# Parting the two gathers of a unit, and turning the last y term by term

## The chip, the cores and the metric

The kernel runs on one core of one Trainium2 chip. The metric is the device time of a whole execution in microseconds; the median of three runs stands for a kernel.

## The reference, cut to what matters

Input x has 32 batches of 512 rows with 256 numbers. The output is x plus a state-space layer plus a mixture of experts, both on the normalised rows xn.

```python
xn = layernorm(x)                                     # [32, 512, 256]
# state-space layer, N = 16 states, L = 512 steps
delta, B, C = split(xn @ W_deltaBC.T, [64, 80])
delta = softplus(delta @ W_dt.T + b_dt)               # [32, 512, 256]
h[t, n] = exp(delta[t] * A[n]) * h[t-1, n] + delta[t] * B[t, n] * xn[t]
y[t] = sum over n of h[t, n] * C[t, n]  +  D * xn[t]
# mixture of experts: each of 8 experts takes its best K = 128 rows of each batch
G, I = top_k(softmax(xn @ Wg.T) transposed, 128)
ex = xn[I]                                            # gather
out_e = G * (gelu(ex @ W1 + b1) @ W2 + b2)
result = x + y + scatter_add(out_e at I)
```

## The kernel before, in words

A first stage normalises the rows, writes them to HBM (`xn_rows`), projects them, and picks each expert's 128 rows of every batch. Then a main loop runs over 32 batches. Each batch is cut into 4 units (quarters 0 to 3, `sl` in the code) of `STEPS` = 4 states; so there are 128 units u. In each unit the state-space work on 4 states of one batch and the expert work on one pair of row sets (`UB` = 2, that is 2 x 128 rows of one expert) go on side by side. Each engine has its own instruction list in a fixed order, tied to the others by semaphores.

- **DVE** (`main`, lines 997 to 1008): for each state a scan over time (`tensor_tensor_scan`), then the multiply `du` x B of the next state into `bank_x` (L936, `multiply_b`), then the product of this state's h with C into `prod` (L1008). The products of states 4 and 8 are POOL's (L573).
- **POOL**: adds each product into `ysum` (L585, at most some states behind the DVE; a product buffer is free again when its sum is done), forms `delta` (L517) and `du` (L523) for the next batch in quarter 3, issues the gathers of unit u+3 (`gather`, L509), the two scatters of unit u-1 (`scatter`, L540) and the addition of a finished batch's y to the output (`add_y`, L554). The rows of an issued gather land in `ex[:, u % 2]`.
- **PE**: in unit u, with v = u+1 and a counter q from 0 to 7: up products of unit v (`up`, L1163) at q = 0 to 3; at q = 3, ahead of `up(v, 3)`, `chosen_columns(v + 1, ...)` (L1082) turns the gathered rows of unit u+2 into `bank_t`, and waits for both gathers of it; down products of unit u (L1229) at q = 4 to 7. At q = 4 and q = 6 it spreads B over the partitions for the states 4sl+3 and 4sl+4 (L1116, `spread_b`). It turns the y of the batch before (`y_rows`, L1110), the xn rows (L1090) and the rank product (L1073).
- **ACT**: copies B for the states 4sl+1 and 4sl+2 into `bank_b` (L748), scales the experts' output (`og`, L757), gelus (L726, pairs 0 to 3), copies the turned rows to `ext` (L741, between pairs 2 and 3, waiting for `chosen_columns`), exp and ln of the softplus in quarter 2 (L697, L701), and the `decay` factors of the next unit (L717).
- **SP**: loads C for the next unit (`c_all`), B (`b_wide`), weights, xn rows, with `held(...)` waits in a fixed order.

The end: in the unit behind the last one (u = `NU`) PE turns the y of the last batch in two halves of 16 matmuls each, four terms per tile (`ysum`, `kept`, `skip` and the last product), into `bank_t` and `bank_x`; ACT and DVE copy one half each, POOL adds it to the output. The order on POOL within the last unit is written out by hand in `main`.

Of the kernel before, what the change touches and what calls it, by code (L numbers as in the profile page):

```python
# [35 lines left out]
P = 128  # L36
# [42 lines left out]
def build(nc, x, wdbc, wdt, bdt, alog, dpar, wg, w1, b1, w2, b2, out):  # L79
    ctx = ExitStack()  # L80
    with ctx:
# [371 lines left out]
        def _(pool):  # L453
# [50 lines left out]
            def gather(u):  # L504

                wait(pool, ex_tr, u - 1)
                pool.wait_ge(picks_done, 2 + u // 64 * 2)
                for i in range(UB):
                    pool.indirect_dma_start(  # L509
                        out=ex[:, u % 2, i], out_offset=None, in_=xn_rows,  # L510
                        in_offset=bass.IndirectOffsetOnAxis(ap=idx_all[:, u * UB + i:u * UB + i + 1], axis=0),
                    ).then_inc(gathered[u % 2], 16)
# [12 lines left out]
            for v in range(2):  # L525
                gather(v)
            take_delta(1, 0)
            take_du(1, 0, 16)
            gather(2)
# [26 lines left out]
            def main(j):  # L556
                for k in range(BU):
# [6 lines left out]
                    for i in range(STEPS):  # L564
# [25 lines left out]
                        if i == 0:  # L590
                            if there(u + 3, NU):
                                gather(u + 3)
# [5 lines left out]
                        if i == 2 and u == NU - 1:  # L598
                            scatter(u, 1)
                            scatter(u, 0)  # L600
# [229 lines left out]
        def _(dve):  # L830
# [184 lines left out]
            nc.vector.tensor_copy(yrow[:, (NB - 1) % 2, 2:4], bank_x[:, 0, 0:T].rearrange("p (c d) -> p c d", c=2)).then_inc(yrow_done, 1)  # L1015
# [3 lines left out]
        def _(pe):  # L1019
# [79 lines left out]
            def y_rows(par, half, last=False):  # L1099

                into = bank_x[:, 0, 0:T] if last and half else bank_t[:]
                for c in (2 * half, 2 * half + 1):
                    for dt in range(HC):
                        part = into[:, (c % 2) * D + dt * P:(c % 2) * D + (dt + 1) * P]
                        rows = slice(c * P, (c + 1) * P)
                        terms = [ysum[:, par, dt, rows], kept[:, par, dt, rows], skip[:, par, dt, rows]]
                        if last:
                            terms.append(prod[:, STEPS - 1, dt, rows])
                        for t, term in enumerate(terms):
                            o = nc.tensor.matmul(part, term, ident[:], start=(t == 0), stop=(t == len(terms) - 1), is_transpose=True)  # L1110
                o.then_inc(y_tr, 1)

# [60 lines left out]
            def main(j):  # L1173
                for k in range(BU):
# [3 lines left out]
                    for q in range(2 * STEPS):  # L1178
# [64 lines left out]
                        if q in (5, 6) and u == NU:  # L1243
                            pe.wait_ge(yrow_done, NB * 2 - 2)
# [40 lines left out]
```

## Time and profile before

| | before |
|---|---|
| runs, median (lowest to highest) | 2426.65 us (2425.75 to 2430.33) |
| profiled execution, its own time | 2422.32 us |
| its span, first to last instruction | 2420.4 us |
| mean granted TensorE clock | 0.987 of full speed |
| busy: PE / DVE / ACT / POOL | 2286.8 / 2349.7 / 2074.3 / 2146.5 us |
| issue to landing of a gather / a scatter / y's addition | 2.8 / 5.2 / 8.5 us, medians |
| PE's waits for gathered rows at L1082 | 9.2 us, once (at 160.3 us, in the start) |

Busy time is the sum of the lengths of an engine's instructions. A timeline line reads: start, length, engine, line of the kernel, operation, what it writes and reads, how many instructions were merged, and in square brackets the idle time before it with what ended it. Lengths of neighbouring instructions overlap by some tenths, since the next one starts up while one drains. PEclk is the share of the TensorE clock's full speed of 2.4 GHz that was granted; 0.50 is the lower level of 1.2 GHz.

### The profile page before, as it was taken

What the parts mean: (1) busy time and instruction counts of PE and PEld (TensorE: products, weight loads), DVE (VectorE), ACT (ScalarE), POOL (GpSimd) and SP (SyncE); (2) the same over time, 40 slices, a digit from 0 to 9 for tenths busy, and PEclk for the clock granted to TensorE, in tenths of its full rate; (3) what the DMA queues carried; (4) which work ended last, traced back from release to release, by engine and by line L of the source; (5) the groups of instructions that cost most, each with busy time, mean ns of one, the idle gap of its engine ahead of it and who ended that gap; (6) DMA issues with size and microseconds to landing.
All of it is one profiled execution on the core that took longest, in us unless ns stands there. A gap on an engine that the chain in (4) does not pass through costs nothing. (4 is left out here: it accounts for less than half of the span.)

```text
span 2420.4 us, 33772 instructions
## 1 busy us (share of the span) xinstructions
PE 2286.8 (94%) x10756; PEld 1816.4 (75%) x10756; DVE 2349.7 (97%) x1975; ACT 2074.3 (86%) x3629; POOL 2146.5 (89%) x1235
## 2 busy tenths in 40 slices
PE   7749999999999999999999999999999999999996
PEld 4437777777777777777777777777778777777775
DVE  5799999999999999999999999999999999999997
ACT  7748889898888888988888889888898989888884
POOL 5527999999999899999999999999999999999997
PEclk9969999999999999999999999999999999999998
DMA  9967575645656565555656555565646456565444
GB/s 344 338 209 266 158 221 157 177 136 148 168 147 173 145 161 141 165 154 134 184 137 173 136 166 145 141 176 143 177 127 180 127 151 163 149 173 139 128 127 79
DMA packets 151649, 403.04 MB, mean 167 GB/s; under 512 B 19536, under 2 KB 88240, under 8 KB 134832
## 3 DMA queue, kind: packets, MB, share of 16 engines
q1 hardware_dynamic: 84208, 316.72, 38.2%
q0 software_dynamic: 66048, 83.92, 20.6%
q8 instruction: 87, 1.43, 0.2%
q14 instruction: 90, 0.74, 0.1%
q10 hardware_dynamic: 1216, 0.23, 0.0%
HBM read 323.72 MB, written 91.75 MB: 172 GB/s over the span
## 5 line engine op out<-in xcount | busy, mean ns | idle before, releaser
L585 POOL TENSOR_TENSOR ysum<-ysum,prod 128x1024 f32<-128x1024 f32 x415 | 1121.4, 2702 | 20.3 <-DVE prod L1008 12.1
L997 DVE TENSOR_TENSOR_SCAN bank_x<-decay,bank_x 128x1024 f32<-128x1024 f32 x448 | 1024.7, 2287 | 8.9 <-DVE bank_x L936 0.5
L1163 PE MATMUL bank_l<-ext,w_sb 128*128 128x256 f32 x4096 | 968.9, 384 | 28.2 <-ACT og L757 22.6
L1229 PE MATMUL bank_l<-w_sb,hid 128*128 128x256 f32 x4096 | 939.0, 382 | 0.0
L1163 PEld LDWEIGHTS bank_l<-ext,w_sb 128*128 128x128 f32 x4096 | 760.3, 191 | 166.5 <-ACT og L757 31.0
L1229 PEld LDWEIGHTS bank_l<-w_sb,hid 128*128 128x128 f32 x4096 | 767.5, 190 | 130.0 <-issue 29.0
L717 ACT ACTIVATE decay<-delta,a_sb 128x511 f32<-128x511 f32 x1024 | 641.9, 707 | 15.8 <-POOL delta L517 14.6
L936 DVE TENSOR_TENSOR bank_x<-du,bank_b 128x1024 f32<-128x1024 f32 x512 | 617.6, 1206 | 4.7 <-ACT bank_b L748 3.2
L726 ACT ACTIVATE hid<-bank_l,b_all 128x256 f32<-128x256 f32 x1024 | 431.5, 475 | 203.8 <-PE bank_l L1163 200.7
L1008 DVE TENSOR_TENSOR prod<-bank_x,c_all 128x1024 f32<-128x1024 f32 x448 | 544.9, 1216 | 0.1
L540 POOL DMA_INDIRECT out<-og,idx_all x256 | 410.0, 1601 | 43.8 <-POOL ysum L585 42.5
L509 POOL DMA_INDIRECT ex<-xn_rows,idx_all x256 | 258.5, 1010 | 109.4 <-issue 61.4
L748 ACT COPY bank_b<-b_wide 128x512 f32<-128x512 f32 x256 | 153.5, 599 | 7.2 <-DVE bank_x L936 6.2
L757 ACT ACTIVATE og<-bank_l,gate_all 128x256 f32<-128x256 f32 x256 | 105.9, 464 | 32.6 <-PE bank_l L1229 32.5
L1116 PE MATMUL bank_b<-bcs,pick 96*128 96x512 bf16 x256 | 98.5, 385 | 31.0 <-DVE bank_x L936 30.0
L717 ACT ACT_TABLE_LOAD x97 | 124.5, 1283 | 1.7
L824 ACT ACT_TABLE_LOAD x95 | 121.9, 1283 | 1.7
L573 POOL TENSOR_TENSOR prod<-zabs,c_all 128x1024 f32<-128x1024 f32 x32 | 109.5, 3421 | 0.0
L1116 PEld LDWEIGHTS bank_b<-bcs,pick 96*128 96x128 bf16 x256 | 24.8, 97 | 99.6 <-DVE bank_x L936 51.7
L573 POOL TENSOR_TENSOR kept<-kept,c_all 128x1024 f32<-128x1024 f32 x32 | 92.6, 2893 | 0.0
L1082 PE MATMUL bank_t<-ident,ex 128*128 128x128 f32 x512 | 77.3, 274 | 9.2 <-DMA ex<-xn_rows,idx_all 9.2
L741 ACT COPY ext<-bank_t 128x512 f32<-128x512 f32 x128 | 76.1, 594 | 6.1 <-PE bank_t L1082 6.1
(117 smaller groups left out, 1958.9 us busy)
## 6 DMA issues: line engine op xcount, KB each, us to landing
c_all<-bc_rows SPq DMA_DIRECT2D x128, 1024.0 KB, 5.1
b_wide<-bc_rows SPq DMA_DIRECT2D x128, 512.0 KB, 4.5
w_sb<-in_w SPq DMA_DIRECT2D x32, 1024.0 KB, 9.3
decay<-in_x SPq DMA_DIRECT2D x32, 512.0 KB, 6.8
xn_rows<-c_all SPq DMA_DIRECT2D x32, 512.0 KB, 6.5
out<-yrow POOLq DMA_DIRECT2D x32, 512.0 KB, 8.5
xr<-xn_rows SPq DMA_DIRECT2D x30, 512.0 KB, 6.0
bc_rows<-prod SPq DMA_DIRECT2D x32, 192.0 KB, 5.1
```

The costliest lines, as they stand in the source:

```text
L509: pool.indirect_dma_start(out=ex[:, u % 2, i], out_offset=None, in_=xn_rows, in_offset=bass.IndirectOffsetOnAxis(ap=idx_all[:, u * UB + i: ...
L540: pool.indirect_dma_start(out=out_rows, out_offset=bass.IndirectOffsetOnAxis(ap=idx_all[:, w * UB + c:w * UB + c + 1], axis=0), in_=og[:, ...
L573: nc.gpsimd.tensor_tensor(to, from_, c_all[:, u % 2, i][:, None, :].broadcast_to([P, HC, T]), ALU.mult).then_inc(gp_prod_done, 1)
L585: nc.gpsimd.tensor_tensor(ysum[:, m % 2], first, prod[:, i], ALU.add).then_inc(sum_done, 1)
L717: nc.scalar.activation(decay[:, par, i, dt, 1:T], delta[:, dpar_, dt, 1:T], ACT.Exp, scale=a_sb[:, dt, n:n + 1]).then_inc(decay_done, 1)
L726: nc.scalar.activation(hid[:, k % 2, f], bank_l[(pair + k) % 2][:, (f % 2) * UT:(f % 2 + 1) * UT], ACT.Gelu_apprx_tanh, bias=b1_all[:, exp ...
L748: nc.scalar.copy(bank_b[:], b_wide[:, s % STEPS - WIDE[0]]).then_inc(b_ready, 1)
L936: nc.vector.tensor_tensor(bank_x[:, s % 2].rearrange("p (c t) -> p c t", c=HC), du[:, par], bank_b[:][:, None, :].broadcast_to([P, HC, T]) ...
L997: nc.vector.tensor_tensor_scan(into, decay[:, k % 2, i].rearrange("p c t -> p (c t)"), bank_x[:, s % 2], 0.0, ALU.mult, ALU.add).then_inc( ...
L1008: nc.vector.tensor_tensor(prod[:, i], bank_x[:, s % 2].rearrange("p (c t) -> p c t", c=HC), c_all[:, u % 2, i][:, None, :].broadcast_to([P ...
L1163: i = nc.tensor.matmul(bank_l[(q + v) % 2][:, (f % 2) * UT:(f % 2 + 1) * UT], w1_sb[:, e2, hc, f * P:(f + 1) * P], ext[:, v % 2, hc], star ...
L1229: i = nc.tensor.matmul(o, hid[:, w % 2, f, c * K:(c + 1) * K], w2_sb[:, w_par, f], start=False, stop=(f == FC - 1 and c == UB - 1))
```

## The change

Three things are altered. `gather(u)` becomes `gather(u, i)` and issues one of the two gathers; in the main loop gather 0 of unit u+3 stands behind the first sum of a unit (as both did), and gather 1 behind the last sum (i = 3), ahead of `add_y` where there is one. In the last unit the scatters of the unit itself, which both stood behind sum 14, are parted: scatter 1 stands behind sum 13, scatter 0 behind sum 14. And the last y is turned term by term: `last_term` turns one term of one half, in the order skip, kept, `ysum`, last product, each term behind its own wait; the second half goes to `bank_l[0]` instead of `bank_x`, from where DVE copies it.

```diff
--- before.py
+++ after.py
@@ -501,15 +501,14 @@
             for r in range(4):
                 pool.wait_ge(rows_out[r], 16 * NB // 4)
 
-            def gather(u):
+            def gather(u, i):
 
                 wait(pool, ex_tr, u - 1)
                 pool.wait_ge(picks_done, 2 + u // 64 * 2)
-                for i in range(UB):
-                    pool.indirect_dma_start(
-                        out=ex[:, u % 2, i], out_offset=None, in_=xn_rows,
-                        in_offset=bass.IndirectOffsetOnAxis(ap=idx_all[:, u * UB + i:u * UB + i + 1], axis=0),
-                    ).then_inc(gathered[u % 2], 16)
+                pool.indirect_dma_start(
+                    out=ex[:, u % 2, i], out_offset=None, in_=xn_rows,
+                    in_offset=bass.IndirectOffsetOnAxis(ap=idx_all[:, u * UB + i:u * UB + i + 1], axis=0),
+                ).then_inc(gathered[u % 2], 16)
 
             def take_delta(nb, par):
 
@@ -523,10 +522,12 @@
                 nc.gpsimd.tensor_tensor(du[:, par], delta[:, par], xnt[:, par], ALU.mult).then_inc(du_done, 1)
 
             for v in range(2):
-                gather(v)
+                for i in range(UB):
+                    gather(v, i)
             take_delta(1, 0)
             take_du(1, 0, 16)
-            gather(2)
+            for i in range(UB):
+                gather(2, i)
             split_rest(NG - 1)
             split_lo(NG - 1)
             y_before = {}
@@ -587,17 +588,15 @@
                             take_delta(b + 2, (m + 1) % 2)
                             wait(pool, bx_done, b * N)
                             take_du(b + 2, (m + 1) % 2, (j * 2 + (m + 1) // 2 + 1) * 16)
-                        if i == 0:
-                            if there(u + 3, NU):
-                                gather(u + 3)
+                        if i in (0, 3) and there(u + 3, NU):
+                            gather(u + 3, i // 3)
                         if i in (1, 2) and there(u - 1, NU) and u < NU - 1:
                             scatter(u - 1, i - 1)
                         if i == 0 and u == NU - 1:
                             scatter(u - 1, 0)
                             scatter(u - 1, 1)
-                        if i == 2 and u == NU - 1:
-                            scatter(u, 1)
-                            scatter(u, 0)
+                        if i in (1, 2) and u == NU - 1:
+                            scatter(u, 2 - i)
                         if i == 3 and sl == 0 and there(b - 2, NB) and u < NU:
                             add_y(b - 2, u)
                         if i == 3 and sl == 2 and b == NB - 1:
@@ -1012,7 +1011,7 @@
             through(main, NJ)
             dve.wait_ge(y_tr, NB * 2)
             dve.wait_ge(y_added, (NB - 2) * 16)
-            nc.vector.tensor_copy(yrow[:, (NB - 1) % 2, 2:4], bank_x[:, 0, 0:T].rearrange("p (c d) -> p c d", c=2)).then_inc(yrow_done, 1)
+            nc.vector.tensor_copy(yrow[:, (NB - 1) % 2, 2:4], bank_l[0].rearrange("p (c d) -> p c d", c=2)).then_inc(yrow_done, 1)
 
 
         @block.tensor
@@ -1096,19 +1095,26 @@
                 pe.wait_ge(gp_prod_done, gp_prods(y * N + N))
                 pe.wait_ge(skip_done, y + 1)
 
-            def y_rows(par, half, last=False):
-
-                into = bank_x[:, 0, 0:T] if last and half else bank_t[:]
+            def y_rows(par, half):
+
                 for c in (2 * half, 2 * half + 1):
                     for dt in range(HC):
-                        part = into[:, (c % 2) * D + dt * P:(c % 2) * D + (dt + 1) * P]
+                        part = bank_t[:, (c % 2) * D + dt * P:(c % 2) * D + (dt + 1) * P]
                         rows = slice(c * P, (c + 1) * P)
-                        terms = [ysum[:, par, dt, rows], kept[:, par, dt, rows], skip[:, par, dt, rows]]
-                        if last:
-                            terms.append(prod[:, STEPS - 1, dt, rows])
-                        for t, term in enumerate(terms):
-                            o = nc.tensor.matmul(part, term, ident[:], start=(t == 0), stop=(t == len(terms) - 1), is_transpose=True)
+                        for term in (ysum, kept, skip):
+                            o = nc.tensor.matmul(part, term[:, par, dt, rows], ident[:],
+                                                 start=(term is ysum), stop=(term is skip), is_transpose=True)
                 o.then_inc(y_tr, 1)
+
+            def last_term(term, half, first=False, last=False):
+
+                into = bank_l[0] if half else bank_t[:]
+                for c in (2 * half, 2 * half + 1):
+                    for dt in range(HC):
+                        o = nc.tensor.matmul(into[:, (c % 2) * D + dt * P:(c % 2) * D + (dt + 1) * P],
+                                             term[:, dt, c * P:(c + 1) * P], ident[:],
+                                             start=(first and c % 2 == 0 and dt == 0), stop=(last and c % 2 == 1 and dt == HC - 1), is_transpose=True)
+                return o
 
             def spread_b(s, n, par):
 
@@ -1240,13 +1246,22 @@
                             if 0 < b < NB - 1 and sl == y_slot(b, 0):
                                 y_ready(b - 1)
                                 y_rows((m - 1) % 2, 0)
-                        if q in (5, 6) and u == NU:
+                        if q == 5 and u == NU:
+                            par = (NB - 1) % 2
                             pe.wait_ge(yrow_done, NB * 2 - 2)
+                            pe.wait_ge(og_done, NU * UB)
+                            pe.wait_ge(skip_done, NB)
+                            for half in range(2):
+                                last_term(skip[:, par], half, first=True)
+                            pe.wait_ge(gp_prod_done, gp_prods(NB * N))
+                            for half in range(2):
+                                last_term(kept[:, par], half)
                             pe.wait_ge(sum_done, sums(NB * N) - 1)
-                            pe.wait_ge(gp_prod_done, gp_prods(NB * N))
+                            for half in range(2):
+                                last_term(ysum[:, par], half)
                             pe.wait_ge(prod_done, dve_prods(NB * N))
-                            pe.wait_ge(skip_done, NB)
-                            y_rows((NB - 1) % 2, q - 5, True)
+                            for half in range(2):
+                                last_term(prod[:, STEPS - 1], half, last=True).then_inc(y_tr, 1)
 
             through(main, NJ)
```

## Rows read from the trace of the kernel before

**Rows 1.** Windows, one batch: start:end us, length, busy PE PEld DVE ACT POOL, PEclk, DMA.

```profile
1170.02:1239.42 69.40, 67.76 (x321) 54.68 (x320) 69.10 (x48) 61.78 (x109) 65.03 (x36) 1.00 0.53 140
```

**Rows 2.** Waits from 300 to 2300 us: waiter, waited for, total us, times, longest.

```profile
DVE bank_x L936 <- ACT bank_b L748: 2.0, 6, 0.7
POOL ysum L585 <- DVE prod L1008: 1.9, 3, 1.6
```

**Rows 3.** Timeline, DVE: start us, length us, instruction; products 3 and multiplies 13, 14, 4.

```profile
1170.02 1.22 DVE L1008 TENSOR_TENSOR prod<-bank_x,c_all 128x1024 f32<-128x1024 f32 x1
...
1207.07 1.21 DVE L936 TENSOR_TENSOR bank_x<-du,bank_b 128x1024 f32<-128x1024 f32 x1
1208.18 1.22 DVE L1008 TENSOR_TENSOR prod<-bank_x,c_all 128x1024 f32<-128x1024 f32 x1
...
1211.64 1.23 DVE L936 TENSOR_TENSOR bank_x<-du,bank_b 128x1024 f32<-128x1024 f32 x1
...
1238.31 1.21 DVE L936 TENSOR_TENSOR bank_x<-du,bank_b 128x1024 f32<-128x1024 f32 x1
1239.42 1.22 DVE L1008 TENSOR_TENSOR prod<-bank_x,c_all 128x1024 f32<-128x1024 f32 x1
```

**Rows 4.** Timeline, POOL: sum 7, delta, second gather, sum 15, sum 3.

```profile
1193.78 2.89 POOL L585 TENSOR_TENSOR ysum<-ysum,prod 128x1024 f32<-128x1024 f32 x1
...
1214.74 2.36 POOL L517 TENSOR_TENSOR delta<-delta,zabs 128x1024 f32<-128x1024 f32 x1
...
1221.08 0.98 POOL L509 DMA_INDIRECT ex<-xn_rows,idx_all  x1 [0.31 <-issue]
...
1229.88 2.89 POOL L585 TENSOR_TENSOR ysum<-ysum,prod 128x1024 f32<-128x1024 f32 x1
...
1243.71 2.89 POOL L585 TENSOR_TENSOR ysum<-ysum,prod 128x1024 f32<-128x1024 f32 x1
```

**Rows 5.** Instructions that write tile ex, 300 to 2330 us: issue to landing.

```profile
DMA to landing us min/median/max: 2.7/2.8/4.2
```

**Rows 6.** Timeline, PE: turned rows (quarters 2 and 0), spreads 3 and 4.

```profile
1193.70 0.60 PE L1082 MATMUL bank_t<-ident,ex 128*128 128x128 f32 x4
...
1227.99 0.60 PE L1082 MATMUL bank_t<-ident,ex 128*128 128x128 f32 x4
...
1230.69 0.39 PE L1116 MATMUL bank_b<-bcs,pick 96*128 96x512 bf16 x1 [0.38 <-DVE bank_x L936]
...
1236.19 0.38 PE L1116 MATMUL bank_b<-bcs,pick 96*128 96x512 bf16 x1
```

**Rows 7.** Timeline of the end: POOL, then PE, then DVE.

```profile
2402.09 2.34 POOL L585 TENSOR_TENSOR ysum<-ysum,prod 128x1024 f32<-128x1024 f32 x1 [0.46 <-DVE prod L1008]
2404.58 1.55 POOL L540 DMA_INDIRECT out<-og,idx_all  x1 [0.15 <-issue]
...
2413.10 1.36 POOL L554 DMA_DIRECT2D out<-yrow  x1 [5.12 <-DVE yrow L1015]
...
2405.80 0.45 PE L1110 MATMUL bank_t<-ident,ysum 128*128 128x128 f32 x1 [8.91 <-DVE prod L1008]
...
2411.87 0.69 DVE L1015 COPY yrow<-bank_x 128x512 f32<-128x512 f32 x1 [6.33 <-PE bank_x L1110]
```

**Rows 8.** Timeline, ACT: last gelus of quarter 2, B copies of states 13, 14.

```profile
1196.07 0.84 ACT L726 ACTIVATE hid<-bank_l,b_all 128x256 f32<-128x256 f32 x2 [0.85 <-PE bank_l L1163]
...
1205.93 0.60 ACT L748 COPY bank_b<-b_wide 128x512 f32<-128x512 f32 x1
...
1210.99 0.62 ACT L748 COPY bank_b<-b_wide 128x512 f32<-128x512 f32 x1
```

**Rows 9.** Timeline, PE: sixteen up products behind two idle times.

```profile
877.52 3.72 PE L1163 MATMUL bank_l<-ext,w_sb 128*128 128x256 f32 x16 [1.57 <-ACT og L757]
...
1989.60 5.41 PE L1163 MATMUL bank_l<-ext,w_sb 128*128 128x256 f32 x16 [2.20 <-ACT og L757]
```

**Rows 10.** Windows, columns as in rows 1: the stretch behind the longer idle.

```profile
1991.00:1994.00 3.00, 3.00 (x8) 2.38 (x8) 3.00 (x3) 1.60 (x4) 2.83 (x3) 0.50 0.57 115
```

## The prediction

> **What bounds the kernel now.** I read one steady batch first, then the waits, then the timelines of the four engines side by side. Names: quarters 0 to 3 are the four units of four states in a batch; sum 7 is the POOL addition of state 7; multiply 14 is the DVE's `du` times B of state 14. In one batch of 69.4 us the DVE is busy for 69.1 us [rows 1]. Over 2000 us of steady work it waits only 2.0 us for ACT, and POOL waits 1.9 us for the DVE's products [rows 2]. The same product recurs after 69.40 us (1170.02 and 1239.42) [rows 3]. So the DVE sets the time and nothing else shows, but PE (67.8 us busy of 69.4) and POOL (65.0 us plus the gaps of 0.15 to 0.3 us between its instructions) are nearly as full [rows 1]. A change that holds one of these two up comes through quickly. A change that only frees them a little brings nothing, because the DVE has no wait to lose.
>
> **Part 1: the second gather moves from behind the first sum of a quarter to behind its last.** Who needs it: POOL in unit u gathers for unit u+3; PE in unit u turns the rows of unit u+2, behind the up products of q = 2 and ahead of those of q = 3. So what POOL gathers in one unit is needed by PE in the next. Before, the second gather of quarter 3 was issued at 1221.08 [rows 4] and, with the 2.8 us that a gather takes to land [rows 5], was there at 1223.9, 4.1 us ahead of PE's transposes at 1227.99 [rows 6]. The move puts three sums and two scatters between, some 10 us. That is more than the cover. POOL cannot pay for it by running ahead, since its sums need the DVE's products. So I work out the cycle with POOL as early as its data let it be; s is a shift against the timeline of before.
>
> *Quarter 1's gather, needed by PE in quarter 2.* Product 3 ends at 1239.42 + 1.22 = 1240.64 [rows 3]; call this E. Sum 3 can start 0.1 us behind it and takes 2.34 us when alone [rows 7], so it ends at E + 2.4. In the trace sum 3 starts at 1243.71, and sum 7 of the same batch, one period behind the row at 1193.78, at 1263.18 [rows 4]: 19.47 us, with the pair of gathers of quarter 1 between. Now there is one gather of that pair less (0.98 us and its gap of 0.31 [rows 4], 1.3 us), and the second gather of quarter 0 more (1.0 us and a gap, 1.2 to 1.4 us). Sum 7 ends at E + 21.8, its gather starts 0.17 us later (the gap of a DMA behind a sum [rows 7] is 0.15) and lands 2.8 us after that, at E + 24.8, and PE can start at 1265.6. It started at 1193.70 + 69.40 = 1263.10 [rows 6]. So s = 2.5 us.
>
> *Who is queued behind it.* On PE, the eight products of q = 3 and the spread of B for the last state of the quarter. On ACT, the copy of the turned rows and the gelu at 1196.07, which already waited 0.85 us for PE. From there to the B copies of states 13 (1205.93) and 14 (1210.99) ACT runs without a gap: tables, exp, decays, ln, gelus [rows 8]. Multiply 14 starts at 1211.64, 0.03 us after that copy ends [rows 3, 8]. So that chain has no reserve, and all 2.5 us arrive at multiply 14. Multiply 13 started 0.5 us after its copy ended (1206.53 to 1207.07), so it and product 12 are 2.0 us late.
>
> *Quarter 3's gather, needed by PE in quarter 0 of the next batch.* Product 12 ends at 1208.18 + 1.22 + 2.0 = 1211.4 [rows 3], sum 12 at 1213.8. Before, delta started (sum 12 ended) at 1214.74 and sum 15 ended at 1229.88 + 2.89 = 1232.77 [rows 4]: 18.0 us, now 1.3 us less for the gather that has left: 1230.5. Plus 0.2, 2.8 and 0.1 us: PE can start at 1233.6 instead of 1227.99 [rows 6]. PE is 5.6 us late, though it had only been 2.5 us late till then: it stands idle for about 3 us.
>
> *What of this arrives at the DVE.* PE had 0.38 us of waiting to give away at 1230.69 [rows 6], so 5.2 us are left. The spread for state 4 ended at 1236.19 + 0.38 = 1236.57 [rows 6], and multiply 4 started at 1238.31 [rows 3]: 1.7 us of reserve. Multiply 4, and product 3 right behind it, come 3.5 us late. Product 3 is E of the next batch, so 3.5 us is the loss of each batch with PE at full speed. In the next batch PE starts 5.2 - 3.5 = 1.7 us late, which still covers the gather of quarter 0 (it lands at E + 2.4 + 0.2 + 2.8 = 1246.0), and waits 0.8 us in quarter 2. The gather of quarter 2 is not late. POOL must wait about a microsecond at sum 12 and at sum 3, so the assumption that its data bind it holds.
>
> *The clock.* After an idle of 2.20 us the sixteen products at 1989.60 took 5.41 us; after one of 1.57 us the same sixteen at 877.52 took 3.72 [rows 9]. Behind the longer one, from 1991 to 1994, the granted clock was 0.50, the 1.2 GHz level [rows 10]. The idle of about 3 us in quarter 0 is longer than either, so I take it that the clock falls behind it, and price it by these rows at 5.41 - 3.72 = 1.7 us. This comes wholly on the chain to multiply 4: 3.5 + 1.7 = 5.2 us for a batch. The Trainium skill, "TensorE: Matmul & The Clock Gate", section "HAM oscillation — how this bites in real kernels", tells of a kernel whose every tile waits for a DMA and starts again at the low clock. By that rule this change makes such a kernel of this one, with the fall at each wait of about 3 us, and its sum would be the 161 us below; the rows at 1989.60 agree with it once, and those at 877.52 show a shorter wait that did not do it.
>
> *Count.* Quarter 1 and quarter 3 have both gathers in the 31 batches 0 to 30: 31 x 5.2 = 161 us. Bounds: the landing varied from 2.7 to 4.2 us [rows 5], and gather 2 now starts near the 512 KB load of `b_wide`; each 0.1 us more is 3 us in all. Below, only the 2.5 us of quarter 2 arrive: 78 us. Above, the 0.8 us wait also drops the clock: 6.9 us a batch, 214 us. I stay at 5.2, by the rows of the idle of 2.20 us, the nearest one.
>
> *POOL's own account.* Each of the 125 units loses a gap of 0.31 us between the gathers and gains one of 0.15 to 0.17, and two waits that are long satisfied. Priced at nothing, because POOL ends up waiting for products; without that cover it would be worth at most 0.15 us x 125 = 19 us, and only if POOL bounded. SP's queue gets no instruction; its loads follow the DVE's products and shift with them.
>
> **Part 2: the end.** Before, PE turned all 32 tiles behind the last product: the first at 2405.80, the copy behind the last at 2411.87 [rows 7], 6.07 us, 0.19 each. Skip and kept (16 tiles) now go ahead. 8 tiles of `ysum` wait for sum 14, and 8 remain behind the product. But scatter 1 of the last unit (1.55 us and a gap) now stands ahead of sum 14, which had waited only 0.46 us and ended at 2404.43 [rows 7]. It ends at about 2405.7. Two groups of 8 follow at 0.2 us a tile, to 2409.0: a gain of 2.8 us. Were the sum not late, 4.4. I take 3 us, all on the path, as the write of y at 2413.10 waited 5.12 us for the copy [rows 7].
>
> **The sum.** Profiled execution 2422.3 (span 2420.4) + 161 - 3 = 2580. The median of the runs is 4.3 us above the profiled one, and some 2 us of the small waits of before [rows 2] disappear under the new ones: 2582.
>
> **The rivals.**
> 1. The clock stays high. The idle of 1.57 us did not move it, and products stand on either side of each wait. 31 x 3.5 = 109 us: 2426.65 + 109 - 5 = 2530. Chance 0.25.
> 2. Both waits of a batch drop the clock, or the landing is near 4 us beside other loads: 2426.65 + 214 - 5 = 2635. Chance 0.09.
> 3. The loss is paid once: the first late gathers hold the DVE up, POOL gains those microseconds and from then on is always early enough. For it: POOL and DVE have the same period. Against it: even with no wait at any product the cycle above does not close within 69.4 us. Price 3 to 5 us less the 3 of the end: 2428. Chance 0.05.
> 4. Faster. The gathers come in time because PE arrives at its transposes later than I read, then only the end (up to 4.4 us) and the small waits of the DVE (2.0 us) count: 2426.65 - 6.4 = 2420. It decides at the landing: it would have to be 2.4 us sooner in quarter 2 and 3.1 us sooner in quarter 0. Chance 0.02.
> The forecast has 0.59.
>
> **How the numbers follow.** Forecast 2582. The range goes from 2505 (2.5 us a batch and a little) to 2640 (6.9 us a batch) and leaves out rivals 3 and 4 and some of the edges of 2. A measurement of this kernel can tell 0.2%, 4.9 us, from no change: faster 0.02, same 0.05, slower 0.93.
>
> **What would show it.** PE waits for the DMA of `ex` at L1082, twice a batch, about 0.8 and 3 us, some 110 us in all or more. The DVE waits for `bank_b`: for ACT at states 13 and 14 and for PE at state 4. The period from product 3 to product 3 is about 74.6 us. The granted clock shows falls once a batch. POOL waits for products. At the end 8 tiles stand behind the last product. Wrong would be: a period of 69.4 us; waits at L1082 spread over all four quarters; a longer period with the DVE waiting for POOL's sums instead.

## The result and the profile after

The changed kernel takes 2716.41 us (median, 2708.33 to 2718.6), before takes 2426.2 us beside it: the ratio is 1.1188, with an interval of 1.116 to 1.1215. It is 290 us slower. The forecast was 2582 us, and the range ended at 2640: the sign and the place were right, the size was not.

The page of the changed kernel: the span, busy time with its share, the granted clock by slices, and three of the costliest groups (busy, mean ns | idle before them and what ended most of it).

```profile
span 2716.5 us, 33895 instructions
...
PE 2374.7 (87%) x10756; PEld 1864.8 (69%) x10756; DVE 2375.1 (87%) x1975; ACT 2080.8 (77%) x3629; POOL 2147.1 (79%) x1235
...
PEclk9979989999999999999899999989999999989999
...
L586 POOL TENSOR_TENSOR ysum<-ysum,prod 128x1024 f32<-128x1024 f32 x415 | 1054.8, 2542 | 312.7 <-DVE prod L1007 307.3
...
L935 DVE TENSOR_TENSOR bank_x<-du,bank_b 128x1024 f32<-128x1024 f32 x512 | 622.8, 1216 | 278.6 <-PE bank_b L1122 201.8
...
L1081 PE MATMUL bank_t<-ident,ex 128*128 128x128 f32 x512 | 93.2, 313 | 253.1 <-issue 234.7
```

Before, DVE was busy for 97% of the span. Now it is 87%, in much the same microseconds. The idle time before L935 (L936 of before), 278.6 us, is almost the whole loss, and PE's spreads of B (L1122) ended most of it. PE, too, was busy for 2374.7 us instead of 2286.8, with the same 10756 matmuls: some of them ran slower. The waits from 300 to 2600 us say who waited for whom (total us, times, longest); they answer to [rows 2].

```profile
POOL ysum L586 <- DVE prod L1007: 311.9, 152, 11.2
...
PE bank_t L1081 <- issue: 221.9, 71, 12.4
...
DVE bank_x L935 <- PE bank_b L1122: 187.5, 59, 10.7
DVE bank_x L935 <- ACT bank_b L747: 65.7, 172, 1.3
```

POOL, which waited 1.9 us for products before, now waits 311.9 us, so it did not bound anything. PE stood 221.9 us at L1081, the turned rows; the trace names no releaser there ("issue"), but the batch below shows what ended it. DVE waited for PE (187.5) and for ACT (65.7), the two that were forecast. Over the 29 batches of this window the forecast had 29 x 2.7 = 78 us for PE (1.0 us and the clock's 1.7 a batch) and 29 x 2.5 = 73 us for ACT: ACT's part was about right, PE's was more than double.

One pair of batches. First DVE: three scans of state 4 in a row (the period), and its longer waits in the second of them, at states 13, 14, 3 and 4. They answer to [rows 3].

```profile
1479.57 2.28 DVE L996 TENSOR_TENSOR_SCAN zabs<-decay,bank_x 128x1024 f32<-128x1024 f32 x1
...
1555.38 2.28 DVE L996 TENSOR_TENSOR_SCAN zabs<-decay,bank_x 128x1024 f32<-128x1024 f32 x1
...
1593.42 1.23 DVE L935 TENSOR_TENSOR bank_x<-du,bank_b 128x1024 f32<-128x1024 f32 x1 [0.55 <-ACT bank_b L747]
...
1598.49 1.23 DVE L935 TENSOR_TENSOR bank_x<-du,bank_b 128x1024 f32<-128x1024 f32 x1 [0.52 <-ACT bank_b L747]
...
1626.05 1.23 DVE L935 TENSOR_TENSOR bank_x<-du,bank_b 128x1024 f32<-128x1024 f32 x1 [5.24 <-PE bank_b L1122]
...
1631.55 1.23 DVE L935 TENSOR_TENSOR bank_x<-du,bank_b 128x1024 f32<-128x1024 f32 x1 [0.94 <-PE bank_b L1122]
...
1633.82 2.28 DVE L996 TENSOR_TENSOR_SCAN zabs<-decay,bank_x 128x1024 f32<-128x1024 f32 x1
```

The two periods are 75.8 and 78.4 us, where before had 69.4. The forecast was 74.6 for all. Then PE, with its rows of quarter 0 (1543.33 and 1621.64) and of quarter 2 (1580.53), which answer to [rows 6], and the eight up products behind one of them:

```profile
1543.33 1.04 PE L1081 MATMUL bank_t<-ident,ex 128*128 128x128 f32 x4 [4.74 <-issue]
...
1580.53 0.63 PE L1081 MATMUL bank_t<-ident,ex 128*128 128x128 f32 x4 [0.77 <-issue]
...
1621.64 1.08 PE L1081 MATMUL bank_t<-ident,ex 128*128 128x128 f32 x4 [6.91 <-issue]
1622.52 3.28 PE L1169 MATMUL bank_l<-ext,w_sb 128*128 128x256 f32 x8
```

POOL's second gathers of quarter 3 are these (they answer to 1221.08 in [rows 4]):

```profile
1539.46 1.01 POOL L508 DMA_INDIRECT ex<-xn_rows,idx_all  x1 [0.16 <-issue]
...
1615.03 1.01 POOL L508 DMA_INDIRECT ex<-xn_rows,idx_all  x1 [0.16 <-issue]
```

From issue to PE's start it is 3.87 us in the first batch (1539.46 to 1543.33) and 6.61 us in the second (1615.03 to 1621.64). The prediction had put in 2.9. SP's queue shows what is different in the second:

```profile
1614.39 0.33 SPq L404 DMA_DIRECT2D b_wide<-bc_rows  x1
1614.76 0.43 SPq L305 DMA_DIRECT2D w_sb<-in_w  x1
1615.24 0.47 SPq L309 DMA_DIRECT2D w_sb<-in_w  x1
```

The load of the wide B and both halves of the next expert's weights are issued within one microsecond around the gather: the first two ahead of its start at 1615.03, the last 0.2 us behind it. Over all batches, issue to PE's start in quarter 0 is 10.2 to 11.5 us in batches 1 to 3, then 3.7 to 4.8 us in one batch and 6.6 to 8.1 us in the next, in turn, as weights are loaded in every second batch; the mean of batches 1 to 31 is 6.1 us. Quarter 2's is 2.9 to 4.1 us behind the first three batches, and its wait 0.8 to 1.0 us in most batches, which is what was forecast. From batch 1 on, PE's idle times ahead of the turned rows add up to 204 us in quarter 0, where about 3.1 x 31 = 96 were forecast, to 25 us in quarter 2, where 0.8 x 31 = 25 were, and to 13 us in the two other quarters together.

Then the clock behind a wait of 4.65 us (two windows: length, busy times, then PEclk; and two rows of PE), answering to [rows 9] and [rows 10]:

```profile
1383.90:1390.00 6.10, 6.02 (x16) 4.06 (x17) 3.11 (x2) 2.05 (x4) 3.91 (x2) 0.50 0.21 24
...
1390.20:1393.60 3.40, 3.40 (x10) 2.72 (x10) 3.31 (x2) 3.39 (x6) 2.20 (x1) 0.56 0.03 5
...
1384.86 3.62 PE L1169 MATMUL bank_l<-ext,w_sb 128*128 128x256 f32 x8
...
1389.38 5.60 PE L1235 MATMUL bank_l<-w_sb,hid 128*128 128x256 f32 x16
```

The low level lasted for the whole 6.1 us of the first window and for most of the second: the trace has it from 1383.0 to 1393.2. The eight up products took 3.62 us instead of 1.89, and sixteen down products 5.60 instead of 3.72. The forecast had priced only the first of these two groups (1.7 us). Between 250 us and the last 70 us the trace has 31 low stretches, about one a batch, of 3.4 to 13.7 us, and PE was busy for 165 us in them. And the end, which answers to [rows 7]:

```profile
2703.88 1.12 PE L1114 MATMUL bank_t<-ident,ysum 128*128 128x128 f32 x4 [7.11 <-POOL ysum L586]
...
2706.49 1.02 PE L1114 MATMUL bank_l<-ident,prod 128*128 128x128 f32 x4
...
2702.45 1.23 DVE L1007 TENSOR_TENSOR prod<-bank_x,c_all 128x1024 f32<-128x1024 f32 x1
2707.55 0.69 DVE L1014 COPY yrow<-bank_l 128x512 f32<-128x512 f32 x1 [3.87 <-PE bank_l L1114]
...
2700.90 2.92 POOL L586 TENSOR_TENSOR ysum<-ysum,prod 128x1024 f32<-128x1024 f32 x1
...
2708.79 1.35 POOL L555 DMA_DIRECT2D out<-yrow  x1 [3.25 <-issue]
```

### The profile page after: what moved, and what is told of

Same layout as the page of the kernel before. It is cut to its first block and busy times, and to the rows that moved or that the text cites. A ratio compares the mean times of both kernels' runs of the same rounds, so it can differ in the third digit from the quotient of the medians.

```text
span 2716.5 us, 33895 instructions
## 1 busy us (share of the span) xinstructions
PE 2374.7 (87%) x10756; PEld 1864.8 (69%) x10756; DVE 2375.1 (87%) x1975; ACT 2080.8 (77%) x3629; POOL 2147.1 (79%) x1235
## 5 line engine op out<-in xcount | busy, mean ns | idle before, releaser
L586 POOL TENSOR_TENSOR ysum<-ysum,prod 128x1024 f32<-128x1024 f32 x415 | 1054.8, 2542 | 312.7 <-DVE prod L1007 307.3
L1169 PE MATMUL bank_l<-ext,w_sb 128*128 128x256 f32 x4096 | 1016.3, 397 | 24.4 <-ACT og L756 14.4
L1235 PE MATMUL bank_l<-w_sb,hid 128*128 128x256 f32 x4096 | 954.1, 386 | 0.0
L1169 PEld LDWEIGHTS bank_l<-ext,w_sb 128*128 128x128 f32 x4096 | 793.0, 199 | 174.1 <-issue 23.5
L1235 PEld LDWEIGHTS bank_l<-w_sb,hid 128*128 128x128 f32 x4096 | 778.3, 193 | 138.3 <-issue 31.7
L935 DVE TENSOR_TENSOR bank_x<-du,bank_b 128x1024 f32<-128x1024 f32 x512 | 622.8, 1216 | 278.6 <-PE bank_b L1122 201.8
L508 POOL DMA_INDIRECT ex<-xn_rows,idx_all x256 | 260.1, 1016 | 74.5 <-DVE gate_all L948 20.2
L1081 PE MATMUL bank_t<-ident,ex 128*128 128x128 f32 x512 | 93.2, 313 | 253.1 <-issue 234.7
L1081 PEld LDWEIGHTS bank_t<-ident,ex 128*128 128x128 f32 x512 | 66.2, 158 | 288.7 <-issue 273.5
L586 POOL TENSOR_TENSOR ysum<-prod 128x1024 f32<-128x1024 f32 x32 | 75.0, 2344 | 46.6 <-DVE prod L1007 46.6
L1122 PE MATMUL bank_b<-bcs,pick 96*128 96x512 bf16 x256 | 102.6, 401 | 4.9 <-DVE bank_x L935 4.3
L574 POOL TENSOR_TENSOR prod<-zabs,c_all 128x1024 f32<-128x1024 f32 x32 | 94.4, 2950 | 0.0
```

Source lines behind the costliest of these rows:

```text
L508: pool.indirect_dma_start(out=ex[:, u % 2, i], out_offset=None, in_=xn_rows, in_offset=bass.IndirectOffsetOnAxis(ap=idx_all[:, u * UB + i: ...
L586: nc.gpsimd.tensor_tensor(ysum[:, m % 2], first, prod[:, i], ALU.add).then_inc(sum_done, 1)
L935: nc.vector.tensor_tensor(bank_x[:, s % 2].rearrange("p (c t) -> p c t", c=HC), du[:, par], bank_b[:][:, None, :].broadcast_to([P, HC, T]) ...
L1081: o = nc.tensor.transpose(bank_t[:, hc * UT + i * K:hc * UT + (i + 1) * K], ex[:, k % 2, i, hc * P:(hc + 1) * P], ident[:])
L1169: i = nc.tensor.matmul(bank_l[(q + v) % 2][:, (f % 2) * UT:(f % 2 + 1) * UT], w1_sb[:, e2, hc, f * P:(f + 1) * P], ext[:, v % 2, hc], star ...
L1235: i = nc.tensor.matmul(o, hid[:, w % 2, f, c * K:(c + 1) * K], w2_sb[:, w_par, f], start=False, stop=(f == FC - 1 and c == UB - 1))
```

## The experiments

**The end alone.** The gathers stay as in before.

```diff
-                        if i in (0, 3) and there(u + 3, NU):
-                            gather(u + 3, i // 3)
+                        if i == 0 and there(u + 3, NU):
+                            gather(u + 3, 0)
+                            gather(u + 3, 1)
```

The two waits at the head of `gather` are made for the first of the pair alone, as in before.

> Only the end is changed (last y term by term, the two own scatters of the last unit parted); both gathers of a unit stay behind the first sum. In the trace of the changed kernel the write of the last y was issued 5.1 us behind the last product, 7.56 us before. Theory (the end gains what its chain shows): 2.4 us less than before, about 2424. Rival (a scatter ahead of sum 14 eats the gain): no difference, 2426. Second rival: the end has a part in the loss: above 2430.

Measured: 2420.69 against 2423.13 us, ratio 0.9995 (0.9986 to 1.0004). The medians are 2.4 us apart as the chain says, but the interval holds 1, so the times alone do not show the gain. The trace does: the last y's write is issued 5.2 us behind the last product (DVE 2403.82 + 1.23 to POOL 2410.22), 7.6 us in before.

```profile
2403.82 1.23 DVE L1009 TENSOR_TENSOR prod<-bank_x,c_all 128x1024 f32<-128x1024 f32 x1
...
2410.22 1.36 POOL L556 DMA_DIRECT2D out<-yrow  x1 [3.29 <-issue]
```

The end has no part in the loss: with the gathers left in their old place none of the 290 us is there, so the gathers carry all of it.

**The landing: few weights.** The changed kernel, with later weight loads cut to 16 columns.

```diff
-                sp.dma_start(w1_sb[:, par], w1_tiles[e]).then_inc(w1_in[par], 16)
+                cols = F if free <= 0 else 16
+                sp.dma_start(w1_sb[:, par, :, 0:cols], w1_tiles[e][:, :, 0:cols]).then_inc(w1_in[par], 16)
```

The same was done for w2.

> The changed kernel, but the expert weights of the main loop are loaded only once per buffer; later loads fetch 16 columns, so that the output of later experts is computed with old weights. Theory (in every second batch the 2 MB of weights, issued just ahead of the second gather of quarter 3, delay its landing from 3.8 to 7.3 us): the wait of PE for the rows in quarter 0 is 4.7 us in all batches, 15 x 3.5 = 53 us less and perhaps 5 to 15 us more through the clock: 2650 to 2665. Rival (the weights are innocent, the landing is late for the order in the POOL queue): 2710 or more.

Measured: 2674.87 us, ratio 1.1051 (1.102 to 1.1083). From batch 4 on issue to PE's start in quarter 0 is 3.0 to 5.1 us in every batch, the pattern of two is gone. The gain is 41.5 us (33 by the ratios, 0.0137 of 2425), less than the 51 to 66 expected. From batch 4 on only 13 batches load weights, not 15, and in these issue to PE's start went from 7.4 to 4.6 us on average, 2.8 us and not 3.5: 13 x 2.8 = 36 us. The extra gain through the clock did not show.

**The clock: filled.** The changed kernel, with 32 transposes of the identity ahead of the wait in quarter 0.

```diff
+                if filler:
+                    wait(pe, ext_done, taken)
+                    for _ in range(filler):
+                        nc.tensor.matmul(bank_t[:, 0:P], ident[:], ident[:], start=True, stop=True, is_transpose=True)
                 pe.wait_ge(gathered[k % 2], count)
```

> The changed kernel, with 32 extra transposes of the identity (3.5 us at full clock) put in the PE queue ahead of the wait for the gathered rows in quarter 0, into the bank that the turned rows overwrite. Theory (the clock falls behind the idle of 4.7 us and more, PE was busy for 88 us longer in all): the granted clock stays at 1.00 behind most waits, 50 to 80 us less, 2635 to 2665. Rival (the low clock is hidden under other waits, or the fill delays the rows): 2710 or more.

Measured: 2661.32 us, ratio 1.0984 (1.0964 to 1.1004): 55 us less than the changed kernel (49 by the ratios, 0.0204 of 2425) for doing more work. PE is now busy for 53 us at the lower level where the changed kernel had 165 us. At half speed that is (165 - 53) / 2 = 56 us of PE time given back, by my estimate, so nearly all of it arrives; some 27 us of low clock are left. In the timeline of PE the fill takes 3.66 us, the rows are there 0.18 us later, and the up products behind them run at full speed (1.89 us, not 3.28):

```profile
1511.18 3.66 PE L1080 MATMUL bank_t<-ident 128*128 128x128 f32 x32
1515.02 0.66 PE L1085 MATMUL bank_t<-ident,ex 128*128 128x128 f32 x4 [0.18 <-DMA ex<-xn_rows,idx_all]
1515.51 1.89 PE L1173 MATMUL bank_l<-ext,w_sb 128*128 128x256 f32 x8
```

Behind the first four batches and up to the last two, the periods without weights are now 74.0 to 75.4 us, those with weights 78.7 to 81.3 but for one of 75.8. The rival that the low clock hides under other waits has fallen.

**Both.**

> Both remedies on the changed kernel: the 32 extra transposes ahead of the wait in quarter 0, and only 16 columns of the later weight loads, so that later experts are computed with old weights. With the fill alone the batches without weight loads took 74.3 us, those with them about 79. Theory (late landing behind the weights and the low clock are the two terms that were missing, and they add up): all batches behind the first four at 74 to 75 us, 2661 - 13 x 4.7 = 2600. Rival (the one hides behind the other): 2640 or more.

Measured: 2612.62 us, ratio 1.0799 (1.0772 to 1.0825); from batch 4 on the periods are 73.6 to 77.8 us (72.5 for the last), half of them under 74.5. By the ratios the weights are worth 45 us here (1.0984 - 1.0799) and 33 without the fill: the two remedies do not hide one another. It is 12 us above what was expected. The batches that issue the cut weight loads are still longer, 75 to 78 us in most, than the others at about 74, so the cut loads are not free.

**The copies of the first batches.** As the last, and `residual` fetches 16 of 512 steps in the main loop.

```diff
-                sp.dma_start(out[rows], x[rows]).then_inc(resid_out[part * UB // HALF], 16)
+                steps = T if part < HALF // UB else 16
+                sp.dma_start(out[rows, 0:steps], x[rows, 0:steps]).then_inc(resid_out[part * UB // HALF], 16)
```

> As the kernel with the fill and few weights (2612.6), and in the first four batches the copies of x to the output fetch 16 of 512 steps of each row set, so that half of the output lacks x. In that kernel the periods of the first four batches were 77.6, 85.7, 81.7 and 75.1 us, later ones 74 to 75. Theory (the copies, issued just ahead of the second gather, hold up its landing to 10 us and more): these four at 74 to 76 us, 15 to 22 us less, 2591 to 2598. Rival (the first batches are long for another cause): 2608 or more.

Measured: 2594.75 us, ratio 1.0709 (1.0682 to 1.0736). The periods of the first four batches went from 77.6, 85.7, 81.7 and 75.1 to 76.9, 75.3, 74.9 and 75.0 us. 18 us by the medians and 22 by the ratios, as expected.

**SP's other loads.** As the last, and the loads of C and of the wide B are cut to 16 columns as well.

```diff
-                sp.dma_start(b_wide[:], bc_rows[u // SLOTS:u // SLOTS + 1, first:first + len(WIDE), :]
-                             .broadcast_to([P, len(WIDE), T])).then_inc(bw_in, 16)
+                steps = T if u == 0 else 16
+                sp.dma_start(b_wide[:, :, 0:steps], bc_rows[u // SLOTS:u // SLOTS + 1, first:first + len(WIDE), 0:steps]
+                             .broadcast_to([P, len(WIDE), steps])).then_inc(bw_in, 16)
```

> As the kernel without the copies, and the loads of C and of the wide B fetch 16 of 512 columns after the first ones, so that the states' products are made with old values: SP's queue moves almost nothing in the main loop. Theory (what is left of the term above the forecast, 4.9 against 3.5 us a batch, is the landing of 3.6 to 4.4 us behind the loads of SP, against the 2.9 that was put in): periods near 73, 2424 + 31 x 3.5 = 2533, 2525 to 2555. Rival (the base term of the cycle was mis-sized in itself, 4.9 us without any other traffic): no gain over the kernel before it, 2585 or more.

Measured: 2536.89 us, ratio 1.0465 (1.0443 to 1.0486); periods of 71.9 to 74.3 us behind the first. That is 110 us above before (113 by the ratio), 3.5 us for each of 31 batches: the term that the prediction worked out for the cycle without the low clock, and what it gave for that rival (2530). Issue to PE's start in quarter 0 went from 4.4 us on average in the kernel before it to 3.2 us here (2.8 to 4.4). The order on POOL, with its two scatters ahead of this gather, is the same in both, so it was not these that held up the landing. DVE's waits from 300 to 2500 us, first in the kernel before it, then here (total us, times, longest):

```profile
DVE bank_x L938 <- PE bank_b L1129: 68.5, 57, 4.0
DVE bank_x L938 <- ACT bank_b L750: 66.7, 174, 1.3
```

```profile
DVE bank_x L940 <- ACT bank_b L752: 59.7, 175, 2.6
DVE bank_x L940 <- PE bank_b L1131: 32.0, 40, 1.3
```

This window has 30 batches. The forecast of the cycle alone had 2.5 us a batch for ACT, 75 us, and 1.0 us for PE, 30 us.

**Which quarter.** The changed kernel with quarter 3 as in before, then with only quarter 3 parted.

```diff
-                        if i in (0, 3) and there(u + 3, NU):
-                            gather(u + 3, i // 3)
+                        if i == 0 and there(u + 3, NU):
+                            gather(u + 3, 0)
+                        if i == (0 if sl == 3 else 3) and there(u + 3, NU):
+                            gather(u + 3, 1)
```

The other one has `3 if sl == 3 else 0` in its place.

> The changed kernel, but in quarter 3 both gathers stay behind the first sum; in quarters 0 to 2 they are parted. Theory (only the rows for quarter 2 are late, 2.5 us a batch, and no wait is long enough for the clock): period about 72, 2490 to 2510. Rival (all parted quarters bear alike): three quarters of the loss, about 2640.

> The changed kernel, but only in quarter 3 the gathers are parted. Theory: PE is 3.1 us late plus 1 us of landing, 2.1 us of it are covered, the low clock adds 1.8 and the weights 3.5 to 4.5 in every second batch: 3.8 and 8 us a batch, 2424 + 170 = 2594, 2560 to 2620. Rival (all parted quarters bear alike): a quarter of the loss, about 2500.

Measured: 2579.8 us, ratio 1.0659 (1.0629 to 1.069), for quarters 0 to 2, and 2656.87 us, ratio 1.0971 (1.095 to 1.0993), for quarter 3 alone. Both expectations were missed upwards, and the two losses, 156 and 233 us, make 390 where the whole change lost 290. So they cover one another: in the whole change PE comes late out of quarter 0, and from batch 1 on waits in quarter 1 in only three batches, for 3.2 us in all. With only quarter 3 left as in before it waits there in every batch, 78 us in all. PE's turned rows of one such batch:

```profile
1528.34 0.60 PE L1083 MATMUL bank_t<-ident,ex 128*128 128x128 f32 x4
...
1549.89 0.93 PE L1083 MATMUL bank_t<-ident,ex 128*128 128x128 f32 x4 [3.07 <-issue]
...
1569.98 0.64 PE L1083 MATMUL bank_t<-ident,ex 128*128 128x128 f32 x4 [0.60 <-issue]
...
1587.55 0.63 PE L1083 MATMUL bank_t<-ident,ex 128*128 128x128 f32 x4 [0.51 <-issue]
```

The wait in quarter 1 (1549.89, 3.07 us) is a new one. Its gather was issued on POOL 5.5 us before, and SP had issued C and the three loads of `bcs` in the three microseconds ahead of that:

```profile
1544.41 1.02 POOL L508 DMA_INDIRECT ex<-xn_rows,idx_all  x1
...
1541.84 0.34 SPq L397 DMA_DIRECT2D c_all<-bc_rows  x1
1542.28 1.33 SPq L332 DMA_DIRECT2D bcs<-b_rows  x3
```

The clock fell too, which that expectation had ruled out: the four transposes at 1549.89 took 0.93 us instead of 0.60. In this run 22 of PE's 24 idle times of 1.93 to 3.84 us were followed by a low stretch, and none of the 16 of 1.22 to 1.92 us. With quarter 3 alone PE waited 4.4 to 5.3 us in quarter 0 without weight loads and 7.9 to 8.6 with them, and the low stretches were mostly 10.2 and 6.8 us long in turn. The periods are 75.0 and 78.6 us, a loss of 5.6 and 9.2 where 3.8 and 8 were expected; that expectation, too, had priced the clock at 1.8 us.

**The place.** Behind the second sum, and behind the third.

```diff
-                        if i in (0, 3) and there(u + 3, NU):
-                            gather(u + 3, i // 3)
+                        if i in (0, 1) and there(u + 3, NU):
+                            gather(u + 3, i)
```

The other one has `(0, 2)` and `i // 2` in their places.

> The changed kernel with the second gather behind the second sum of a unit instead of the last. Theory (only lateness costs): it is issued 2.2 us later than before, of 4.1 us of cover in quarter 0, so the time stays within 2420 to 2430, unless the weight loads reach the gather in every second batch, then up to 2445. Rival (parting costs by itself, in waits and gaps on POOL): 2450 or more.

> The changed kernel (all loads whole, no fill) with the second gather behind the third sum of a unit. It is issued 4.2 us earlier than behind the last sum and 4.2 us later than behind the second, which cost nothing. Theory (the loss begins where the 4.1 us of cover end): in quarter 0 PE waits about 4 us in the batches with weight loads, under 1 us in the others; 2460 to 2520. Rival (the loss grows evenly with the place): half of it, about 2570.

Measured: 2424.35 against 2423.51 us behind the second sum, ratio 1.0005 (0.9993 to 1.0018); 2469.65 us behind the third, ratio 1.0178 (1.015 to 1.0207); behind the last 1.1188. So the cost does not grow evenly with the place. Behind the second sum it is at most 2.4 us against the run with the end alone (1.0005 and 0.9995, intervals that overlap); it begins where the cover ends. In the run behind the third sum the wait in quarter 0 is 1.3 to 1.8 us in nearly every batch and not 4 us in every second, as I had expected: the gather is issued ahead of the weights there (at 1460.30, the weights at 1463.63). The mean granted clock is 1.00, rounded:

```profile
300.00:2400.00 2100.00, 2013.35 (x9448) 1614.71 (x9447) 2049.62 (x1362) 1827.80 (x3192) 1917.67 (x1034) 1.00 0.56 151
```

Three batches are different. In two of them the wait was 4.7 and 4.9 us, and the clock was low for 6.8 us each time; in the third it was 2.3 us, and the clock was low for 3.4 us. Behind the waits of 1.3 to 1.8 us it stayed high.

**A third buffer.** The change, but its second gather behind the last sum is that of unit u+4.

```diff
-        ex = sb("ex", [P, 2, UB, D])
+        ex = sb("ex", [P, 3, UB, D])
...
-                        if i in (0, 3) and there(u + 3, NU):
-                            gather(u + 3, i // 3)
+                        if i == 0 and there(u + 3, NU):
+                            gather(u + 3, 0)
+                        if i == 3 and there(u + 4, NU):
+                            gather(u + 4, 1)
```

`gathered` and the indices of `ex` go by three as well, a gather waits for `ex_tr` of one unit earlier, and the second gather of unit 3 is issued ahead of the main loop.

> The changed kernel with three buffers for gathered rows instead of two; the second gather stands behind the last sum as in the change, but is that of unit u+4. Theory (the place in the POOL order costs nothing, only the lateness of the rows does): no waits of PE for rows in the main loop, the period back at 69.4 us, 2422 to 2425. Rival (parting the gathers costs POOL or the DVE time by itself): 2440 or more.

Measured: 2420.44 against 2423.13 us, ratio 0.9986 (0.9977 to 0.9995). All of the loss is gone with the second gather in the same place of POOL's order as in the change. Gathers still land late, up to 10.1 us after their issue from 300 to 2400 us, but now nobody needs them that soon. From 300 to 2400 us PE has no wait for rows, and DVE a single one for `bank_b`:

```profile
DVE bank_x L938 <- ACT bank_b L750: 1.0, 1, 1.0
```

This version is faster than before by 2.7 us by the medians, 0.14% by the ratio, of which the run with the end alone had 2.4 us. Parting the gathers brings nothing that a run here could tell from the end alone.

## Why the prediction was right in kind and wrong in size

- **What bounds, and who needs the second gather:** right. The third buffer takes only the lateness away, and the time is back.
- **The cycle at full clock, 3.5 us a batch:** right in sum, less so in its parts. With SP's traffic and the low clock out of the way 110 us were measured, 31 x 3.5 = 109 forecast. There DVE waited 32.0 us for PE where 30 were forecast, and 59.7 for ACT where 75 were. About half of ACT's part came at the states 5, 6, 9 and 10, 0.2 to 0.3 us each, where the forecast had none; at 13 and 14 it was 0.4 and 0.5 us, not 2.5 together. And PE's gap in quarter 0 was 4.2 us there (3.66 of fill and 0.6 of waiting), not 3.1. That the sum came out so close is in part luck.
- **The landing of quarter 3's gather, taken at 2.8 us:** this step failed. The prediction named 2.7 to 4.2 us as bounds "as the landing varied", and wrote that the gather now starts near the load of `b_wide`, but priced it by the range of a gather that had always been issued elsewhere. Where it stands now, SP has just issued its loads: the wide B, in every second batch 2 MB of weights, in the first batches copies of x. It took 3.7 to 4.8, 6.6 to 8.1 and 10.2 to 11.5 us to PE's start, 6.1 on average, where 2.9 had been put in. By the prediction's own measure, 3 us for each 0.1 us, this alone is about 100 us.
- **The clock, 1.7 us a batch, 53 us:** right that it falls, too low in size. The price came from one event of the trace before, with one group of products at the lower level. Here PE was busy for 165 us in 31 low stretches, 82 us lost at half speed by my estimate, against 53. The fill gave back 55 us (49 by the ratios), which is near 53 only because it removed two thirds of the low stretches.
- **The sum:** with these two terms as they turned out, 2582 + 100 + 29 = 2711, against 2716 measured. This is an estimate. The steps of the runs, by the ratios against before, are 49 us for the fill, 45 for the weights, 22 for the copies, 59 for C and the wide B, and 113 that stay, 288 in all; the last three cuts make 126. Their sizes hang on the order in which the parts are taken away (the weights were worth 33 or 45). And the 126 are not all landing: with the same order, issue to PE's start in quarter 0 went from 6.0 us with the fill alone to 3.2, which is 88 us over 31 batches, and quarter 2's by 0.3, which is 10. Most of the rest can be the low clock that the fill had left, some 27 us, since the last kernel has no low stretch from 250 us on to the last 70.
- **"SP's queue gets no instruction; its loads shift":** true, and it is the sentence behind which the mistake hides. The gather was moved past SP's loads in time, though past none in any list.
- **The gather of quarter 0 is not late:** right for this kernel, because PE comes late. With quarter 3 left alone it was late, by 0.8 to 3.8 us from batch 1 to 30.
- **The end, 3 us:** its trace shows 2.4. Sum 14 ended 2700.90 + 2.92 = 2703.8, 0.1 us behind the product, behind a scatter issued at 2699.90. So all sixteen tiles of `ysum` and the product stood behind the product, as the prediction's sum had it, and not eight, as its list of signs said. They ran at the lower level: four tiles took 1.02 to 1.12 us.
- **The rivals:** high clock (2530) is what the clean version showed, not the real one. "Paid once" and "faster" are refuted by periods of 74 to 87 us in all batches. The second rival named the landing beside other loads, the larger cause, with 0.09 of chance; but it took it at near 4 us, and its 2635 was too low. Its other half, that both waits of a batch drop the clock, is not what happened: there is about one low stretch a batch, and the waits of 0.8 to 1.0 us in quarter 2 did not bring one.

What is open: why the low stretch lasted 10.2 us around the wait of 4.65 us and 6.8 us around the one of 6.91 us. C and the wide B were cut together, so the 59 us are not parted between them. And no run held the clock high with all loads whole, so the 82 us of the clock are worked out and not measured.

## What to carry to other kernels

A prefetch's slack is not the time from landing to use in the old place: when its issue moves, look up which other queue issues in the microseconds around the new place, and take the landing from a transfer that really met such traffic. Where an engine turns late in a cycle through several engines, solve the cycle, since a late step in one stage can cover the next one, and parts tried one by one then cost more than all together. If a wait of TensorE remains, look at the granted clock behind it too, and count every group of products that ran at the lower level, not the first alone. Filling such a wait can be cheaper than leaving it: here it was.

## What the runs showed of the hardware

- An indirect gather of 128 rows that lands in 2.8 us (median before) was ready for PE only 6.6 to 8.1 us after its issue when 2.5 MB of plain loads from SP's queue were issued within one microsecond around it, and after 10.2 to 11.5 us in batches 1 to 3, where copies of x are made as well. With SP's loads cut it was 2.8 to 4.4 us.
- A PE idle time of 4.65 us went with 10.2 us at 0.50; at the one of 6.91 us the eight products behind it took 3.28 us instead of 1.89, and the low stretch was 6.8 us long. With quarters 0 to 2 parted, 22 of 24 idle times of 1.93 to 3.84 us were followed by a low stretch, and none of 16 from 1.22 to 1.92 us; waits of 1.3 to 1.8 us in nearly every batch left the granted clock high behind the third sum.
- This speaks for the rule that the prediction took from the Trainium skill, "TensorE: Matmul & The Clock Gate", section "HAM oscillation — how this bites in real kernels": a wait for a DMA in each round brought a fall in nearly each round. Here there were 31 low stretches in 31 batches, and the run with the fill shows a price of about 50 us for two thirds of them.
- 32 transposes that compute nothing, 31 times, made the changed kernel 49 to 55 us faster.
